# Context weights and context factors in 128-row tiles instead of 16-row tiles

## The reference

```
for W, b in Ws:                                  # three layers, 128 channels each
    Xi = einsum('hjk,bjd,bkd->bhd', Wr, X0, Xi) + b[None, :, None]
    res.append(Xi.sum(axis=2))
z = concatenate(res, axis=1)                     # 512 x 384
h = concatenate([z, dense_ctx], axis=1)          # 512 x 400: 384 + 16 of context
h = maximum(h @ W_top1 + b_top1, 0.0)            # W_top1: 400 x 512
h = maximum(h @ W_top2 + b_top2, 0.0)
y = h @ W_top3
```

## Time and profile before

| | |
|---|---|
| median of 3 runs | 674.93 us (673.24 to 676.68) |
| the profiled execution | 673.4 us |
| its span, first to last instruction | 671.4 us |
| TensorE busy | 658.6 us, 98% |
| VectorE busy | 555.5 us, 83% |
| GpSimd busy | 466.4 us, 69% |
| ScalarE busy | 440.0 us, 66% |
| mean granted TensorE clock | 0.984 of full speed |

### The profile page before, as it was taken

The page is one execution under the profiler, slowest core; times in us unless marked ns, Lnnn a source line. Parts: engine busy times, 40 slices in busy tenths (PEclk is TensorE's granted clock), DMA queues, the critical chain, the costliest instruction groups (busy, mean ns, idle before and its releaser), DMA issues.

```text
span 671.4 us, 11301 instructions
## 1 busy us (share of the span) xinstructions
PE 658.6 (98%) x3070; PEld 525.1 (78%) x3070; DVE 555.5 (83%) x1556; ACT 440.0 (66%) x1449; POOL 466.4 (69%) x376
## 2 busy tenths in 40 slices
PE   7899999999999999999999999999999999999997
PEld 7786777787788777777778777777788877777877
DVE  3669899999973899999995599999996589999860
ACT  2655677687843777777763577777784476877851
POOL 6888888888762688888884478787876366444530
PEclk8899999999998999999999999999999999999989
DMA  6123564130403004040402102213130300300000
GB/s 205 23 51 100 137 224 129 24 112 19 118 18 102 16 8 127 8 128 5 121 16 79 55 3 69 67 48 87 32 105 22 98 17 18 115 1 5 1 2 0
DMA packets 38356, 42.25 MB, mean 63 GB/s; under 512 B 17823, under 2 KB 22548, under 8 KB 38165
## 3 DMA queue, kind: packets, MB, share of 16 engines
q1 hardware_dynamic: 32661, 40.23, 19.8%
q0 software_dynamic: 5632, 1.31, 2.1%
HBM read 8.84 MB, written 0.00 MB: 13 GB/s over the span
## 4 chain that ended last, share of the span: by engine, by line
PE 94%; DMA 2%; DVE 1%; ACT 1%; issue 1%; POOL 0%; SPq 0%; DVEq 0%
PE p_u L800 22%; PE p_u L801 21%; PE p_u L802 21%; PE p_x L775 6%; PE p_tower L823 6%; PE p_g L814 5%; PE p_x L772 2%; PE p_x L770 2%; PE p_x L769 2%; PE p_tower L850 1%; DMA g_all<-w_in 1%; PE p_x L740 1%; PE p_tower L836 1%; PE p_tower L835 1%; PE p_tower L842 1%
## 5 line engine op out<-in xcount | busy, mean ns | idle before, releaser
L455 ACT ACTIVATE prod<-p_u,x0t 128x128 f32<-128x128 f32 x1024 | 289.6, 374 | 101.5 <-PE p_u L802 101.5
L634 DVE SCALAR_TENSOR_TENSOR parts<-p_u,x0t,parts 128x128 f32<-128x128 f32 x1024 | 283.2, 340 | 47.2 <-PE p_u L802 47.0
L800 PE MATMUL p_u<-w1h,x1h 128*128 128x512 f32 (+1 forms) x640 | 288.7, 451 | 0.9 <-ACT x1h L436 0.9
L802 PE MATMUL p_u<-w1h,x1l 128*128 128x512 f32 (+1 forms) x640 | 250.3, 391 | 0.0
L801 PE MATMUL p_u<-w1l,x1h 128*128 128x512 f32 (+1 forms) x640 | 250.2, 391 | 0.0
L333 POOL DMA_INDIRECT emb<-table_in,idx_all x176 | 205.7, 1169 | 50.4 <-issue 47.8
L352 POOL TENSOR_TENSOR parts<-parts,prod 128x512 f32<-128x512 f32 x128 | 176.2, 1377 | 57.7 <-ACT prod L455 44.4
L800 PEld LDWEIGHTS p_u<-w1h,x1h 128*128 128x128 f32 x640 | 121.1, 189 | 37.9 <-issue 8.6
L801 PEld LDWEIGHTS p_u<-w1l,x1h 128*128 128x128 f32 x640 | 121.7, 190 | 35.6 <-issue 10.8
L802 PEld LDWEIGHTS p_u<-w1h,x1l 128*128 128x128 f32 x640 | 120.7, 189 | 26.1
L347 POOL TENSOR_TENSOR parts<-prod 128x512 f32<-128x512 f32 x64 | 83.3, 1302 | 73.1 <-ACT prod L455 72.3
(11 more groups left out here) (84 smaller groups left out, 392.1 us busy)
## 6 DMA issues: line engine op xcount, KB each, us to landing
fac_b<-xx SPq DMA_DIRECT2D x90, 234.0 KB
fac_a<-xx SPq DMA_DIRECT2D x45, 78.0 KB
emb<-table_in,idx_all POOLq DMA_INDIRECT x176, 2.8
g_all<-w_in SPq DMA_DIRECT2D x3, 832.0 KB, 6.5
w<-w_in SPq DMA_DIRECT2D x1, 2496.0 KB, 9.4
xx<-xx SPq DMA_DIRECT2D x30, 78.0 KB
fac_b<-xx SPq DMA_DIRECT2D x15, 156.0 KB
bd<-x0t SPq DMA_DIRECT2D x120, 10.0 KB
```

Of the source, the lines that this page charges most:

```text
L455: last = nc.scalar.activation(dst[:, i * H:(i + 1) * H], u[:, i * H:(i + 1) * H], ACT.Copy, scale=x0t[:, par, t, j:j + 1])
L634: nc.vector.scalar_tensor_tensor(out=chain[i][:, p], in0=u[:, i * H:(i + 1) * H], scalar=x0t[:, par, t, j:j + 1], in1=add, op0=ALU.mult, o ...
L800: nc.tensor.matmul(u, xh, wh, start=True, stop=False)
L802: nc.tensor.matmul(u, xl, wh, start=False, stop=True).then_inc(u_full, 1)
```

## The change

`wt1c` and `ctxt` get 128 partitions. VectorE clears both whole tiles at the start, behind the clearing of `bd` and ahead of the sum of the first layer's weights. SyncE waits for both clearings ahead of the load of `wt1c` and loads the first 16 rows of each tile; the other 112 rows stay zeros. The text of `tower_1_early` is the same; since its tiles have 128 rows now, its context products contract over 128 rows.

```diff
-        wt1c = sb("wt1c", [CTX, TOP1])
+        wt1c = sb("wt1c", [128, TOP1])
...
-        ctxt = sb("ctxt", [CTX, B])
+        ctxt = sb("ctxt", [128, B])
...
+        context_cleared = sem("context_cleared")
...
-                sp.dma_start(wt1c[:], wt1_d[3 * 128:3 * 128 + CTX, :]).then_inc(tower_in, 16)
+                sp.wait_ge(context_cleared, 2)
+                sp.dma_start(wt1c[0:CTX, :], wt1_d[3 * 128:3 * 128 + CTX, :]).then_inc(tower_in, 16)
...
-                    sp.dma_start(ctxt[:, c:MACRO_B:STACK], ctx_d[:, at:at + n], allow_slow_non_contiguous=True).then_inc(tower_in, 16)
-                sp.dma_start(ctxt[:, MACRO_B:B], ctx_d[:, MACRO_B:B]).then_inc(tower_in, 16)
+                    sp.dma_start(ctxt[0:CTX, c:MACRO_B:STACK], ctx_d[:, at:at + n], allow_slow_non_contiguous=True).then_inc(tower_in, 16)
+                sp.dma_start(ctxt[0:CTX, MACRO_B:B], ctx_d[:, MACRO_B:B]).then_inc(tower_in, 16)
...
             nc.vector.memset(bd[:], 0.0).then_inc(bd_cleared, 1)
+            nc.vector.memset(wt1c[:], 0.0).then_inc(context_cleared, 1)
+            nc.vector.memset(ctxt[:], 0.0).then_inc(context_cleared, 1)
             dve.wait_ge(w0_in, 16)
```

## The result

The changed kernel took 665.65 us (median of 4 runs, 664.98 to 666.71), the kernel before 674.10 on the same chip (4 runs, 673.24 to 676.68). The ratio is 0.9886, 95% interval 0.9855 to 0.9917: 1.1% faster. The forecast was 666.7 us in a range of 663.0 to 669.5. The profiled execution took 665.45 us with a span of 663.6, and its mean granted clock was 0.992 where it had been 0.984.

A forecast was written before the change was run, and what follows sets the result against it. TensorE, busy 98% of the span and 94% of the chain, was taken to bound the kernel. Gains of 4.6 + 0.35 + 1.7 = 6.7 us off the profiled 673.4 gave 666.7 us, range 663.0 to 669.5.

The forecast's parts named there:

- Context products in the middle: Three middle towers: nine products from 3.54 to 2.0 us, 1.54 us a tower, 4.6 us gained, bounds 3 and 5.
- The reading that the change of row count costs 0.19 us: TensorE's chain: each change between 128 and 16 rows costs about 0.19 us; the extra time is not in one product kind.
- The end's 0.35 us: Program end: 1.54 us off TensorE, but it then waits 0.9 us for VectorE's last fold; gain 0.35, bounds 0 and 0.45.
- The clock in the middle: Middle tower, 213.5 to 217.5 us: the clock's fall goes with the alternation, 1.7 us gained, bounds 0 and 1.7.
- The clock at the end: From 650.5 us: the fall, costing 2.9 us, left at its present price, gain 0, with 2.9 as the other bound.
- The clearings at no cost: VectorE at the start: two clearings, 1.0 us together, fall into idle time; cost 0, upper bound 1.3 us through the third gather.
- rival B: Program end keeps its full clock too, no run of alternation being in front: 663.8 us, chance 0.17.
- The signs: Expected profile: third gather not at 2.3 us, second layer's weight load no later, runs within a few tenths of each other.
- C: Middle tower: clock falls all the same, brought by the tower's short products, not the row changes; 668.4 us, chance 0.13.
- D: Gain handed back, TensorE reaching a bank or VectorE product too early: 673.0 us, partly back 670 to 672; chance 0.08.
- E: Stall belongs to the switch between two operand pairs, not the row count; nothing gained, 673.4 to 674.7 us, chance 0.04.
- F: 128-row weights replacing others wait for the product before them, 0.93 us a product: 693 us, chance 0.03.

The follow-up runs named there:

- E5: Kernel before with 16-row tiles, the four z1 products first and the four context products behind them; 678.53 us, ratio 0.9893 to the kernel before.
- E6: Changed kernel with context products over rows 0 to 63 of the 128-row tiles; 686.05 us in one run, 5.04 us in each middle tower.
- E7: Changed kernel with context products over rows 0 to 95 of the 128-row tiles; 677.64 us in one run, 3.49 us in each middle tower.
- E3: Changed kernel with the two clearings moved earlier, directly behind that of x0t; 677.97 us (7 runs), ratio 0.9887 to the kernel before.
- E4: Changed kernel run again, on another chip; 677.15 us (6 runs), ratio 0.9866 to the kernel before.
- E9: Changed kernel with the eight early products of each tower run twice, all with 128 rows; 683.31 us in one run.
- E10: Changed kernel with 16-row context products in the last tower alone; 676.88 us in one run.
- E1: Kernel before run again, unchanged, on other chips than the first comparison; 685.17 us (12 runs), ratio 1.0002.
- E2: Changed kernel with context products back on rows 0 to 15 of the 128-row tiles, clearings and wait kept; 685.11 us, ratio 0.9995 to the kernel before.
- E11: Changed kernel with the eight early products of each tower run twice and context products over 64 rows; 697.46 us in one run.
- E12: Kernel before with z1 products first, then each 16-row context product four times, sixteen in a row; 692.68 us in one run.

## Why the prediction was right, and where it was not

The likeliest case was off by 1.05 us (665.65 for 666.7). That is partly luck: two of its terms were at nothing and came out at 2.88 and -1.57 us, and more than half of the one cancelled in the other. Its own working has to be judged by the ledger, which has 7.9 us where the sum had 6.7.

- Context products in the middle, 4.6 us: right. 3 x 1.54 us in the trace, 5.03 to 3.49 us a tower, all of it kept; the stretches between the towers are the same within 0.05 us. ScalarE's wait for the last L847 shrank from 5.4 to 3.8 us around the third tower and VectorE's longest wait for a quad from 4.3 to 3.2; neither was used up, as expected.
- The reading that the change of row count costs 0.19 us, and not the 16-row product: shown by E5 (two changes for eight: 3.88 us) and bounded by E6 and E7.
- The end's 0.35 us and the new wait on the fold of about 0.9: 0.35 and 0.96. Right.
- The clock in the middle, 1.7 us: the trace has 3.14 - 1.54 = 1.6. Right in size, and no trace with 128 rows fell in a middle tower (after, E3, E4, E9, E10: 15 towers), while those of the kernel before, E1 and E2 did in 2 of 9.
- The clock at the end, forecast as unchanged: wrong, 2.88 us. The step that failed was "0.9 us of idling takes its place": I treated idling and 16-row products as alike to the clock. They are not. After the change TensorE idles about 0.96 and 0.53 us within 2.3 us and keeps its clock in every trace with this end (after, E3, E4, E7); E10 brings the fall back with 16-row products in the last tower alone. That was rival B, with a chance of 0.17, and it is what happened. Its 663.8 us were not reached because of the slower first macro.
- The clearings at no cost: E2 bears it out within 1.6 us. They took 0.48 us each, as estimated, and the gathers beside them 0.99 and 1.00; the fourth gather, beside the sum of the weights, took 1.63 in place of 0.99. The changed kernel's trace did lose 1.57 us ahead of the first tower, a term that the sum did not have. My later theory that the clearings shift VectorE against the gathers found no support in E2 and E3. What is seen is that VectorE's fp32 work took longer beside GpSimd's sums (0.29 to 1.16 us; 2.67 to 3.79), and that the same program ends this part up to 1.65 us apart. What sets from run to run which instructions meet was not settled.
- The signs: the third gather kept 1.00 us, and the load of the second layer's weights was issued at 9.02 us (9.50 before). The runs were not within a few tenths of each other: the four lie 1.7 us apart, as wide as a fall, and the slowest (666.71) has a mean clock of 0.990 against 0.992. Where it lost that was not traced, so a fall in a middle tower of that run is not excluded.
- The mechanism of the clock was half right. I tied the falls to alternation; E11 and E12 show that the small row count matters and that stalls alone do not do it. That stalls make a fall likelier is suggested by the kernel before and E5, and not shown. Nothing in the prediction's sum rested on the difference, since the change removes both, but a reader who padded to 64 rows would have kept the stalls and lost only the falls.
- Rivals: C (falls all the same) did not occur in a trace, D (gain handed back) neither, E is refuted by E6 and E7 (the same operands in the same order, 64 rows stall and 96 do not), F by the chain of the changed kernel (0.22 us a product).

The Trainium skill's "TensorE: Matmul & The Clock Gate", Part 3, section "The mechanism", has weight loads overlap only between different row groups, though the same section of the Trainium skill also names a background weight buffer as a target that loads are pulled ahead to. The first rule is not borne out for these products: 128 behind 128 rows adds 0.22 us, 96 rows among 128 the same, and 16 or 64 rows among 128 cost 0.41. Nor did it favour the 16-row product, as the prediction had it, since rows 0 to 15 are among those of the 128-row products. The Trainium skill's "TensorEngine Tiling (Array Packing)", section "Available Configurations", lists tilings of 128, 64 and 32 rows; that 96 rows go with 128 and that 64 and 16 stall agrees with modes of these sizes and with the drain that its "Key Properties" name; a change costs 0.19 us here.

## What to carry to other kernels

Where products over few rows stand between full ones, look at the distance from start to start and not at the recorded length: each change into or out of products over 16 or 64 rows cost 0.19 us here, while filling the rows up to 96 or 128 with zeros cost nothing on TensorE. Either fill up, or put all the narrow products together; both gained about 1.1% here. In the change the stalls were worth 5.0 us and the falls of the clock 4.5. The end of the program deserves its own reading of the trace: taking the eight changes away gained 0.35 us there and 1.54 in a middle tower, and a fall of the clock cost 2.9 us there and 1.6 in the middle.

## What had not been expected of the hardware

- Whether the granted clock fell went with how many rows the products used. In the stretches around the middle towers TensorE was recorded as busy throughout in E11 and E12; sixteen changes between 128 and 64 rows kept 2.4 GHz, sixteen 16-row products in a row did not in three of four towers (clock 0.88, 1.00, 0.88 and 0.72 in the four stretches).
- A wait of 0.96 us and one of 0.53 us close together did not lower the clock, where about 3 us of alternating 16-row products with no recorded gap did at the end.
- The same kernel took 674.1 us on one chip and 682 to 687 us on others, nearly all of the difference ahead of the first tower: in E1's trace the execution is 10.9 us longer and the first tower begins 10.5 us later. What it comes from is open; in that trace ScalarE stands still for 4.57 us in the first macro.
- VectorE's subtraction of 128 columns (L582, L584 in the changed kernel) waits out GpSimd's sums. Of its 42 executions between 20 and 80 us in the 14 traces, 28 took 0.34 to 1.76 us, and each of them ended 0.14 to 0.17 us behind the end of a sum of GpSimd's (L347 or L352; L349 or L354). The other 14 took 0.29 us, six of them beside the issue of a gather. The Trainium skill's "SBUF — State Buffer", section "SBUF: two separate sides", describes a port pair that VectorE and GpSimd hold in turns for a whole instruction; the 28 ends agree with that, though no run moved a sum.
